# Sparse cross attention and a routed 16-expert FFN on one core: expert 1's weights requested ahead of the first slot lists, and a threshold search with four corrections

## The reference, cut to what matters

```python
# x: 4 batches x 512 tokens x 512;  ctx_512: 4 x 512 x 128
h = ctx_512
sim = sum over 4 heads of (h Wq^T)(h Wk^T)^T, scaled          # 4 x 512 x 512
threshold = the 153rd largest value of each row of sim          # int(512 * 0.3) = 153
A = sigmoid(sim) * (sim >= threshold);  A = (A + A^T) / 2
x = x + (1 - gamma) * layernorm(x) + gamma * A
xn = layernorm(x)
logits = xn @ router_weight^T + router_bias
top 4 of 16 experts for each of the 2048 tokens, softmax of their logits
y_e = (clip(up)+1) * gate*sigmoid(1.702 gate),  gate_up = xn @ gate_up_proj[e] + bias
x = x + sum over the 4 experts of score * (y_e @ down_proj[e] + down_bias[e])
```

## Time and profile before

| | us |
|---|---|
| median of 3 runs | 894.6 |
| lowest, highest | 886.27, 897.5 |
| the profiled execution | 891.88 |
| its span, first to last instruction | 890.0 |
| PE busy in the span | 773.8 (87%) |
| DVE, ACT, POOL busy | 595.0, 403.4, 318.3 |
| chain that ended last: PE, ACT, DMA, POOL | 65%, 11%, 9%, 5% of the span |

### The profile page before, as it was taken

The page is one execution under the profiler, slowest core; times in us unless marked ns, Lnnn a source line. Parts: engine busy times, 40 slices in busy tenths (PEclk is TensorE's granted clock), DMA queues, the critical chain, the costliest instruction groups (busy, mean ns, idle before and its releaser), DMA issues.

```text
span 890.0 us, 16748 instructions
## 1 busy us (share of the span) xinstructions
PE 773.8 (87%) x3566; PEld 626.6 (70%) x3567; DVE 595.0 (67%) x1068; ACT 403.4 (45%) x663; POOL 318.3 (36%) x351
## 2 busy tenths in 40 slices
PE   4464737469899999999999999999999999999993
PEld 2134436357688888788888887878788878888882
DVE  4678789777567657677575857767766485775541
ACT  3998697532335225425253443543442254352221
POOL 1330657747232323334232332323432333232231
PEclk9765565559899999999999999999999999999997
DMA  8501121156553633674636647467547353723231
GB/s 277 208 0 48 48 49 49 48 175 181 142 133 89 182 69 97 171 214 111 172 102 173 175 97 223 109 174 214 171 108 211 71 159 91 210 66 69 49 61 29
DMA packets 70626, 111.80 MB, mean 126 GB/s; under 512 B 29878, under 2 KB 32182, under 8 KB 70518
## 3 DMA queue, kind: packets, MB, share of 16 engines
q1 hardware_dynamic: 32454, 74.22, 24.4%
q0 software_dynamic: 18336, 36.26, 20.7%
q10 hardware_dynamic: 19728, 0.15, 1.2%
HBM read 83.78 MB, written 28.90 MB: 127 GB/s over the span
## 4 chain that ended last, share of the span: by engine, by line
PE 65%; ACT 11%; DMA 9%; POOL 5%; issue 4%; SPq 2%; DVE 1%; ACTq 1%; DVEq 0%; POOLq 0%
PE gate_up_ps L854 36%; PE bank L854 21%; DMA xg<-xn_rows,gslot 4%; PE bank L836 3%; ACT bgu L520 3%; ACT marks L520 3%; PE bank L844 3%; POOL slot_rows L393 2%; POOL out_dram L437 2%; ACT x_sb L533 1%; DMA bd_raw<-_ffn_down_proj_bias_dram 1%; PE gate_up_ps L743 1%; DMA out_dram<-x_sb 1%; DMA bgu<-n_gate_up_proj_bias_dram 1%; ACT A L530 1%
## 5 line engine op out<-in xcount | busy, mean ns | idle before, releaser
L854 PE MATMUL gate_up_ps<-w,xh 128*128 (+1 forms) x1152 | 365.5, 399 | 0.3 <-DVE xl L1034 0.3
L437 POOL DMA_INDIRECT out_dram<-yb,aslot x72 | 132.6, 1842 | 425.8 <-ACT yb L638 397.1
L854 PEld LDWEIGHTS gate_up_ps<-w,xh 128*128 128x128 f32 x1152 | 213.1, 190 | 41.5 <-issue 0.5
L854 PE MATMUL gate_up_ps<-w,xl 128*128 (+1 forms) x576 | 227.0, 394 | 0.0
L854 PE MATMUL bank<-w,hh 128*128 (+1 forms) x576 | 180.3, 394 | 7.3 <-DVE hl L1039 6.3
L631 ACT ACTIVATE sg<-gc 128x512 f32<-128x512 f32 x72 | 45.6, 634 | 222.5 <-DVE gc L1049 222.5
L1045 DVE TENSOR_TENSOR gu<-gate_up_ps,bgu 128x1024 f32<-128x1024 f32 x72 | 88.2, 1224 | 72.6 <-PE gate_up_ps L854 72.2
L854 PEld LDWEIGHTS bank<-w,hh 128*128 128x128 f32 x576 | 107.8, 189 | 35.3 <-issue 13.4
L1039 DVE TENSOR_TENSOR hl<-bank,hh 128x512 fp32r<-128x512 f32 x72 | 49.6, 688 | 117.1 <-ACT hh L625 117.1
L854 PEld LDWEIGHTS gate_up_ps<-w,xl 128*128 128x128 f32 x576 | 109.2, 190 | 23.7
L625 ACT CAST hh<-bank 128x512 fp32r<-128x512 f32 x72 | 42.3, 587 | 159.9 <-PE bank L844 158.9
(11 more groups left out here) (209 smaller groups left out, 797.6 us busy)
## 6 DMA issues: line engine op xcount, KB each, us to landing
raw_w<-_L_ffn_gate_up_proj_dram SPq DMA_DIRECT2D x64, 512.0 KB, 4.3
raw_w<-in_L_ffn_down_proj_dram SPq DMA_DIRECT2D x64, 256.0 KB, 5.7
bgu<-n_gate_up_proj_bias_dram SPq DMA_DIRECT2D x16, 512.0 KB, 7.1
x_sb<-in_x_dram SPq DMA_DIRECT2D x4, 1024.0 KB, 11.5
xn_rows<-xn SPq DMA_DIRECT2D x4, 1024.0 KB, 5.6
out_dram<-x_sb SPq DMA_DIRECT2D x4, 1024.0 KB, 6.3
xg<-xn_rows,gslot POOLq DMA_INDIRECT x74, 5.4
out_dram<-yb,aslot POOLq DMA_INDIRECT x72, 4.8
```

The source lines that it names most:

```text
L437: pool.indirect_dma_start(out_v, bass.IndirectOffsetOnAxis(aslot[:, k, 0:1], 0), yb[:, k % 2, :], None, bounds_check=TOKENS - 1, oob_is_er ...
L854: last = nc.tensor.matmul(out_ps, lhs[:, rows], w[:, bass.ds(buf, 1), part, c, cols].rearrange("p a d -> p (a d)"), start=(m == 0), stop=( ...
```

## The change

Four edits. The search has four gains in place of five, with other values, and another first quantile; so it has five passes in place of six. The work beside the search that stood at passes 4 and 5 moves to passes 3 and 4. On SP, expert 1's two halves are issued at the head of batch 3's turn, ahead of the wait for the scatters, the slot lists and the store of xn; the wait for the first gather is gone.

```diff
-GAINS = (0.8, 0.7, 0.6, 0.4, 0.3)
+GAINS = (1.0, 0.7, 0.55, 0.32)
 PASSES = len(GAINS) + 1
-QUANTILE, DENSITY = 0.54, 0.345
+QUANTILE, DENSITY = 0.535, 0.345
...
             for b in range(NB):
                 rows = slice(b * N, (b + 1) * N)
                 if b == EARLY:
+                    for h in range(2):
+                        sp.wait_ge(S["lo_done"], HALF * (h + 1))
+                        load_half(1, h, 1)
                     sp.wait_ge(S["scat"], 16 * RT * TOP_K * EARLY)
                     for k in range(FROZEN):
                         sp.dma_start(gslot[:, k, :], slot_d[k * P:(k + 1) * P, :]).then_inc(gslot_in[k], 16)
                         sp.dma_start(aslot[:, k, :], slot_d[k * P:(k + 1) * P, :]).then_inc(aslot_in[k], 16)
                 sp.wait_ge(S["xn2_done"], RT * (b + 1))
                 sp.dma_start(xn_d[rows, :].rearrange("(r p) h -> p r h", p=P), xn2[:]).then_inc(S["xn2_out"], 16)
-                if b == EARLY:
-                    sp.wait_ge(gathered[0], 16)
-                    for h in range(2):
-                        sp.wait_ge(S["lo_done"], HALF * (h + 1))
-                        load_half(1, h, 1)
                 sp.wait_ge(S["bo_done"], RT * (b + 1))
...
                     if it == 2:
                         qk_copy(2)
+                    if it == 3:
+                        scores(2, 0, 2)
                     if it == 4:
-                        scores(2, 0, 2)
-                    if it == 5:
                         scores(2, 2, RT)
                 if b >= 2:
...
-                    if it == 5 and b + 1 < NB:
+                    if it == 4 and b + 1 < NB:
                         ctx_copy(b + 1)
```

## The result

| | us |
|---|---|
| changed kernel, median (lowest to highest) | 897.18 (891.47 to 903.65) |
| kernel before, median of its runs beside them | 891.57 (885.36 to 897.5) |
| ratio, with its 95% interval | 1.0064 (1.0044 to 1.0084) |
| profiled execution, and its span | 896.04, 894.3 |
| profiled execution before, and its span | 891.88, 890.0 |

The change costs 5.6 us between medians and 4.2 us between the two profiled executions. I had forecast +10. So the sign was right and 897.18 lies in the range, but the size was about twice too large. The two traces tell where the size went, if one compares them at a few milestones instead of at their ends. The times are starts of instructions: DVE's split of expert 0, PE's transposes of a tile's gathered rows, and SP's issues. A step is the time from one tile's start to the next one's.

A forecast was written before the change was run, and what follows sets the result against it. PE, 98% busy from 280 to 880 us, bounds the kernel, so only the tiles' start shifts: 5.0 us gained, tile 0 11.4 later, 1.4 back, net 10 slower; 894.6 + 10.0 = 904.6, own range 897 to 912, 8-in-10 893 to 914.

The forecast's parts named there:

- The mechanism: On SP, the slot lists stand behind two landing waits of expert 1's load, so tile 0 begins 11.4 us later.
- The hold: On SP, two landing waits of 6.3 and 6.05 us plus issues put the first list at 195.0 instead of 187.39.
- The list's landing: First slot list on SP's queue, just behind chunk 3, lands in 3.9 us instead of 1.71.
- that rule's sum: Ring order on SP's queue makes the list wait out chunk 3: about 5.6 us, shift 13.1.
- The gather: Tile 0's gather, now behind the store of xn, takes the median 5.4 us instead of 3.76.
- The first phase: Before expert 0's split, one search pass less in each of four batches gains 4.9, say 5.0 us, bounded by 3 and 11.3.
- What comes back: At batch 3's last scatter, transfers no longer under way give back up to 2.0 us, taken as 1.4.
- the prediction's own signs of being wrong: First list issued before 190, split starting before 172 or after 178, or tile 0 late and the end not.
- The first: Rival: the search's first-phase gain is larger, up to 11.3 us, and hides the block; about 893 to 899, chance 0.13.
- The second: Rival: lists and gather wait out chunk 3 and the store of xn; tile 0 19.5 us later, 913, chance 0.08.
- the third: Rival: a row's count ends outside 145 to 152, DVE's slow branch runs, 101 us; about 1006, chance 0.02.
- the fourth: Rival: moving expert 1's load on SP costs nothing, only the search's gain is left; 889.6, chance 0.06.

The follow-up runs named there:

- The load alone: Kernel before with its five corrections kept, only expert 1's load moved ahead of the slot lists on SP; median 898.31 us, ratio 1.0053.
- the search alone: Changed kernel's four-gain search with SP's order of the kernel before, expert 1 loaded behind the lists and first gather; ratio 0.9998 to the kernel before.
- the lists from ACT: Changed kernel plus 32 one-column copies on ACT, with the eight slot lists issued by ACT instead of SP; ratios 0.9920 and 0.9889.
- 32 copies: 32 one-column ACT copies computing nothing, ahead of its loop, added to the changed kernel (1.0024, 1.0007) or to its search with SP's old order (0.9893, 0.9914).
- 216 copies: Kernel before plus 216 one-column copies on ACT ahead of its loop, search and load untouched; one execution, 941.75 us, including the copies' own time.

## Why the prediction was right in sign and wrong in size

**The mechanism: right.** SP's lists wait behind two landings, and from the split to tile 0 it takes 27.9 us instead of 13.5. The load alone repeats it (26.8), the search alone doesn't have it (14.3), and taking the waits or the lists away shortens it (21.9, and 18.3 with the lists from ACT).

**The hold: somewhat too long.** From split to first list I had 195.0 - 175.3 = 19.7 us, and measured were 17.8. SP's two waits took 5.1 and 5.3 us in place of 6.3 and 6.05. I had taken the means of 15 and 14 waits, most of which lie in laps where gathers and adds move too. In this stretch neither moves, and the last chunk's second part landed 3.8 us after its issue. A wait's price should come from a stretch with the same company.

**The list's landing: near, by luck.** 3.45 us (3.56, 3.44 and 3.40 in three other traces with SP's order of the changed kernel) against 3.9. But the 3.9 of the earlier trace rows is no time of lists: it is the median over all 149 transfers that touch `gslot`, 74 gathers among them. ACT's 68 lists alone take 1.9 in the median, and the 8.4 is a gather's:

```profile
gslot<-slot_rows ACTq DMA_DIRECT2D x68, 1.0 KB, 1.9
```

With 1.9 the forecast would have been +8.0. In the changed kernel the first list was issued 0.48 us behind chunk 3's second part. That part landed 3.8 us after 188.66, at about 192.5, and the list at 192.59. The Trainium skill, "DMA: Bandwidth & Descriptors", "Queues, rings and completion order", says that on each DMA engine descriptors are consumed in ring order; the trace agrees, and my price for chunk 3 in that rule's sum (5.6) was too high. The rule is not the only thing at work: on ACT's queue, with no chunk ahead of them, the first three lists for the gathers took 3.50, 5.93 and 5.81 us beside expert 1's chunks. **The gather: right**, 5.70 against 5.4.

**The first phase: mis-sized, 8.96 instead of 5.0.** Search 0 gave 0.4 us and not 0.75, since DVE's aggregate ended at 39.05 and not at 38.65. In search 1 ACT was done at 64.04 (I had 65.15), search 3 ended at 134.6 (I had 138.7), DVE went on from its exponentials at 151.34 (I had 155.5). The step that failed is a reading: "DVE has no wait in this stretch up to 82.98". It had one of 3.83 us, for PE's transposes of A, and it shrank to 1.27, before and after:

```profile
58.63 2.91 DVE L1123 SCALAR_TENSOR_TENSOR x_sb<-gate_up_ps,gam,x_sb 128x512 f32<-128x512 f32 x4 [3.83 <-PE gate_up_ps L799]
```

```profile
55.69 2.91 DVE L1121 SCALAR_TENSOR_TENSOR x_sb<-gate_up_ps,gam,x_sb 128x512 f32<-128x512 f32 x4 [1.27 <-PE gate_up_ps L797]
```

On PE these transposes stand behind batch 2's similarities, and I had let PE's products keep their durations. They did not, before and after:

```profile
53.89 3.78 PE L738 MATMUL bank<-kT,qT 128*128 128x512 f32 x4 [0.68 <-ACT kT L496]
```

```profile
53.16 1.98 PE L736 MATMUL bank<-kT,qT 128*128 128x512 f32 x4 [0.68 <-ACT kT L494]
```

The second case, batch 3's eight, went from 6.12 to 3.79 us. That is the clock: the granted clock was 0.50 in 53 to 57 us before and 1.00 after, the two levels of 1.2 and 2.4 GHz. Over 95 to 112 us it was 0.56 and 0.52 in the kernels with five corrections and 0.79 to 0.80 in all eight with four whose milestones can be compared, and the eight products took 3.79 us in all of these. Over 50 to 62 us it varied among those eight. Five had 0.82 to 0.94, similarities of 1.98 or 1.99 us and a DVE wait of 1.21 to 1.61; the other three had 0.54 to 0.67, similarities of 3.78 us and a wait of 3.83. From the start of these similarities to the split the five took 117.4 to 118.2 us, the three 119.6 to 120.6, the kernels with five corrections 126.1 and 126.4. So the two groups differ by 1.5 to 3.3 us behind that point. The rest of the spread of the splits (169.67 to 176.78) was there before: the similarities began at 52.27 to 56.14, and no run shows why. That the shorter search brings PE's work closer together and so raises the clock is a correlation over these traces. No experiment held the clock, so it is argued and not shown.

**What comes back: mis-sized, 6.0 instead of 1.4.** I had counted the scatter's landing (2.0 at most; it was 4.49 - 2.09 = 2.40) and stopped there. POOL's 16 scatters came 0.7 us closer together and tile 4's list landed 0.6 faster, but its gather 0.4 slower (3.88 against 3.49). The largest part that I left out is PE's clock: after a wait of 1 us and not 4 it stayed at the full one, and the step from tile 4 to 5 gave 11.83 - 9.14 = 2.69 us.

**A step that the prediction lacked: ACT's jump back.** "The stretch of the tiles has the same length" failed. 1.89 and 3.99 us were lost at tiles 66 and 70. The 32 copies bring the changed kernel from 1.0064 (1.0038 when repeated) to 1.0007 and 1.0024, and the search alone from 0.9998 to 0.9914 and 0.9893. The Trainium skill, "Runtime: NRT & Kernel Launch", "Instruction fetch mechanics", says that an engine other than PE holds two blocks of 256 instructions, and that a taken branch to a target outside of them stalls until it is fetched. ACT's loop body has some 300 instructions, an estimate from the trace before: a tile without a split takes at least 35, each of the four splits that it can branch to adds 11, and the body has four tiles. So by that section the jump can find its target or not, depending on where the blocks' borders fall. The traces agree: 74 to 84 or 86 packets and 2.7 to 3.0 us a jump. Which blocks are held at the jump no run shows.

**The sum.** Forecast: -5.0 + 12.6 (hold, 19.7 - 7.1) + 2.2 (list) + 1.6 (gather) - 1.4 = +10.0. Measured: -8.96 + 10.71 + 1.74 + 1.94 - 6.01 up to tile 5, then -1.11 up to tile 65 and +5.88 at the jumps: +4.19. The first phase was off by 4.0 us, the hold by 1.9, what comes back by 4.6 and the tiles behind by 1.1, all in the kernel's favour, and one cost of 5.9 us was missing. That the time fell into the range is partly luck, errors of both signs. Two of the prediction's own signs of being wrong came true: the first list was issued before 190 (189.14) and the split started before 172 (171.33).

**The rivals.** The first (the first phase gains more) came true for its premise, and the time is one of its times, but not by its reason alone: it had all four passes coming through, and what came through was in good part PE's faster products. The second fell with the list's 3.45 us, the third didn't happen (DVE's busy time is 594.6 us, before 595.0), the fourth fell with the hold. Without the loss at the jumps the change is worth nothing measurable, 1.0007 (0.9978 to 1.0036) and 1.0024 (0.9998 to 1.0051): a search worth -0.9 to -1.1% and a hold of the same size or a little more.

## What to carry to other kernels

A queue that executes in order should issue what the critical path is waiting for ahead of any bulk load with landing waits, or that small load should go to an engine that is idle just then; here it turned 1.0007 into 0.9889, and 1.0024 into 0.9920 on another chip. When an edit changes how many instructions an engine has ahead of a loop with more than 256 of them, compare the packets of the instruction queue and the engine's time across the jump before anything else is explained. And a transfer that comes early must be priced at everything it will no longer disturb, PE's clock included.

## What the runs showed of the hardware that was not expected

- A jump back on ACT took 2.25 to 2.26 us in the kernel before, 5.26 to 5.28 in the changed one and 5.01 to 5.28 in the kernel before with 216 copies, with 74, 84 and 86 packets of 8 KB on the instruction queue.
- Behind 3.5 MB of weights issued without waits a scatter of POOL's queue landed in 7.29 and 6.00 us instead of 2.1 to 2.5, and a list of 1 KB in 4.87 and 7.97 instead of 1.7.
- A wait of 4.12 us on PE was followed by products at half speed (1.20 for two), one of 1.01 us was not (0.70).
- With the same first phase, PE's granted clock over 50 to 62 us was anything from 0.54 to 0.94 from kernel to kernel. The way from batch 2's similarities to the split took 117.4 to 118.2 us with the higher clocks and 119.6 to 120.6 with the lower ones.
